# Keeping Silu results in PSUM and fetching a third tree's leaves in a fused attention and tree feed-forward kernel

## The chip, the cores and the metric

The kernel runs on one NeuronCore of one Trainium2 chip. The metric is device time in microseconds (us) of one execution; lower is better. Engines are named as in the profile: PE (matrix multiply), DVE (vector), ACT (scalar), POOL (GpSimd), SP (issues DMAs).

## The reference

Input x is 2 sequences of 4096 tokens, 512 values each. Both layers are preceded by a layer norm and added to x.

```
query, keys, values = unit_projection(LN(x) @ W.T + b)      # fft, divide by |f| + 1e-8, ifft
x1 = x + unbind(cumsum(bind(keys, values), axis=1), query)  # products of spectra
logits = LN(x1) @ W_in.T + b_in          # 8 trees x 255 nodes
decisions = logits > 0                   # one path of 8 nodes per tree
out = x1 + (silu(logits) * on_path) @ W_out.T
```

Each tree has depth 7: 127 inner nodes and 128 leaves. A token walks from the root, right where the decision is 1. Only the 8 nodes on its path count, 7 inner ones and one leaf.

## The kernel before

The 8192 tokens are cut into 32 blocks of 256 tokens (two halves j of 128). In one step of the loop the feed-forward part of block i runs beside the attention part of block n = i + 1 and the layer norm of block n + 1. The loop body (`step`) is written out by hand for each engine, and each engine executes its own list in order; semaphores with counts link them. Nothing is planned at run time: the order in the code is the order of the work.

Attention: PE projects with weights already folded with the Fourier basis (`project`, L485: Q, K, V, each a real and an imaginary part of 24 matmuls into two banks; the next projection may begin a part only when ACT has evacuated it, `evac_re` L724, `evac_im` L731). ACT squares and takes roots (`square`, `root`), POOL adds squares (`sum_squares`), adds the epsilon and later multiplies the spectra: `bind` (four multiplications), then DVE's four scans (`running_sum`, the cumulative sum), then POOL's `unbind` (four), `z_sums` (two), ACT's `z_high` and POOL's `z_low`. PE transforms back (`transform_back`), and DVE folds the result into x1 (`residual`, L1248), computes the statistics and normalises it. ACT's `std` takes the square root of the variance. The transposes of the normalised block are DMAs of SP.

All large products are done with numbers split in two 16-bit parts: high (ACT) and low (DVE), three matmuls for each tile.

Feed-forward: a tree has two column tiles of 128 in the logits: tile 0 holds the inner nodes, tile 1 the leaves. `logits(i, t, c)` (L509) are 12 matmuls of 256 columns into half c of PSUM bank t % 4. DVE's `decide` (L1206) turns tile 0 into decisions; PE's `counts` (L536) adds to the bank, with these decisions and a path matrix, a large negative value for each node that is off the token's path, so that Silu gives 0 there. ACT's `silu` (L787) writes to the buffer `acts` in SBUF, a ring of three trees. `act_high` (L799) rounds that to 16 bits in `a_hi`; DVE's `act_low` (L1216, the instruction is L1220) forms the rest in `a_lo`. `down` (L574) multiplies by W_out for each half into banks 0 and 1, 3 matmuls of 512 columns for each of the 14 tiles. PE may refill a bank when Silu has read it (`act_ready`).

The leaves of trees 0 and 1 are not multiplied. Their counts still run over both tiles, and ACT's `leaf` (L756) makes a one-hot of the leaf from the second half; PE turns it into a row number (`leaf_rows_of`), ACT copies the numbers (`leaf_row_copy`), POOL fetches each token's row of weights, bias and output weights from HBM by indirect DMA (`fetch`, L1051, two DMAs for each tree). DVE's `leaf_dots` (L1225) forms the dot product of the row with the normalised token, ACT's `leaf_silu` (L776) its Silu, and DVE's `leaf_add` (L1237) adds Silu times the output row to x1. `result` (L1278) adds the output of `down`, and SP stores it. GATHERED names these trees; a gathered tree has one tile in `COLUMN`, `a_hi`, `a_lo` and the weights.

A few narrow steps handle the Nyquist term of the spectrum (`nyquist_...`), and `scale_and_shift` (L1112, its second instruction is L1117) makes `nb`, the shift of the next layer norm, from two columns.

## Time and profile before

| | us |
|---|---|
| median of 3 runs (lowest, highest) | 1973.29 (1971.39, 1976.88) |
| the profiled execution, its span | 1974.17, 1972.3 |
| PE busy | 1875.0 (95%) |
| DVE busy | 1659.9 (84%) |
| ACT busy | 1109.8 (56%) |
| POOL busy | 946.3 (48%) |

Busy is time in which an engine had an instruction in work. Matmuls overlap each other, so a busy PE is not one at its peak. The granted clock of PE was 0.987 on the mean over the span.

### The profile page before, as it was taken

The page shows a single profiled execution, that of the slowest core. Times are in us where ns is not written, and L with a number is a line of the kernel's source. Part 1 is how long each engine was busy: PE and PEld are TensorE (multiplying, and loading weights), DVE is VectorE, ACT ScalarE, POOL GpSimd, SP SyncE. Part 2 cuts the span into 40 slices and gives each one's busy share as a digit, 9 for nine tenths or more (in the row PEclk, how much of TensorE's full clock was granted, in tenths as well). Part 3 has the DMA queues.
Part 4 walks back from the last instruction along what each step waited for, and adds up shares of the span by engine and source line. Part 5 has one row for each costly group of instructions (what it writes and reads, how often), then busy time and mean ns, then how long its engine had stood idle before and what let it go on. Part 6 is the DMA issues. An engine that isn't in the chain of part 4 may idle for free.

```text
span 1972.3 us, 40210 instructions
## 1 busy us (share of the span) xinstructions
PE 1875.0 (95%) x14680; PEld 1410.1 (71%) x14680; DVE 1659.9 (84%) x2874; ACT 1109.8 (56%) x2151; POOL 946.3 (48%) x736
## 2 busy tenths in 40 slices
PE   8599999999999999999999999999999999999978
PEld 6477777777777777777777777677777777777755
DVE  4888888888888988888888888888888898887883
ACT  5566555566555556655556655556655555654543
POOL 1254445565444555444556444556544455544450
PEclk9799999999999999999999999999999999999999
DMA  8023223222223222322222222322232322231212
GB/s 278 11 81 92 75 75 96 64 85 85 87 66 92 75 80 80 96 74 75 86 74 83 88 75 75 96 64 85 85 87 66 92 75 80 80 95 56 84 54 65
DMA packets 181784, 163.18 MB, mean 83 GB/s; under 512 B 140160, under 2 KB 140800, under 8 KB 181760
## 3 DMA queue, kind: packets, MB, share of 16 engines
q1 hardware_dynamic: 163328, 95.48, 16.3%
q0 software_dynamic: 18432, 67.38, 11.0%
q8 instruction: 15, 0.25, 0.1%
q14 instruction: 9, 0.07, 0.0%
HBM read 95.72 MB, written 16.78 MB: 57 GB/s over the span
## 4 chain that ended last, share of the span: by engine, by line
PE 69%; DVE 15%; issue 9%; ACT 0%; another core or an unknown queue 0%; DVEq 0%; DMA 0%; SPq 0%; ACTq 0%
PE bank_l L590 29%; PE bank_p L480 24%; PE bank_l L530 10%; DVE arena L1145 5%; DVE dec L1213 3%; DVE arena L1133 2%; PE bank_i L480 2%; PE bank_l L540 1%; DVE arena L1139 1%; DVE arena L1151 1%; DVE arena L1220 1%; PE bank_i L559 0%; PE bank_i L560 0%; PE bank_i L561 0%; PE bank_i L558 0%
## 5 line engine op out<-in xcount | busy, mean ns | idle before, releaser
L530 PE MATMUL bank_l<-arena,win_mem 128*128 128x256 f16 x5376 | 625.7, 274 | 15.4 <-DMA arena<-xn_pair 14.1
L590 PE MATMUL bank_l<-wout_mem,arena 128*128 128x512 f16 x2688 | 590.7, 379 | 0.0
L530 PEld LDWEIGHTS bank_l<-arena,win_mem 128*128 128x128 f16 x5376 | 523.7, 99 | 79.2 <-DMA arena<-xn_pair 14.2
L480 PE MATMUL bank_p<-arena,wf_hi 128*128 128x256 f16 x3072 | 506.1, 273 | 2.3 <-ACT arena L741 2.3
L590 PEld LDWEIGHTS bank_l<-wout_mem,arena 128*128 128x128 f16 x2688 | 263.1, 98 | 303.7 <-issue 0.2
L480 PE MATMUL bank_p<-arena,wf_lo 128*128 128x256 f16 x1536 | 419.2, 273 | 0.0
L985 POOL TENSOR_TENSOR arena<-arena 128x512 f32<-128x512 f32 x96 | 121.8, 1269 | 594.9 <-ACT arena L750 594.9
L795 ACT ACTIVATE arena<-bank_l,bias_in,s_logit 128x256 f32<-128x256 f32 x448 | 227.3, 558 | 208.9 <-PE bank_l L540 202.0
L480 PEld LDWEIGHTS bank_p<-arena,wf_hi 128*128 128x128 f16 x3072 | 299.7, 98 | 37.4 <-ACT arena L741 2.6
L1220 DVE SCALAR_TENSOR_TENSOR arena<-arena,s_act 128x512 f16<-128x512 f32 (+1 forms) x256 | 216.5, 847 | 72.8 <-ACT arena L805 72.8
L1213 DVE TENSOR_SCALAR dec<-bank_l,thr,off 128x256 bf16<-128x256 f32 x256 | 132.6, 538 | 86.8 <-PE bank_l L530 86.2
L1233 DVE SCALAR_TENSOR_TENSOR arena<-arena 128x512 f32<-128x512 f32 x128 | 202.4, 1616 | 0.0
L1062 POOL DMA_INDIRECT arena<-in_leaf_rows,leaf_row x128 | 142.7, 1115 | 88.3 <-issue 56.3
L783 ACT ACTIVATE leaf_act<-leaf_dot,arena 128x1 f32<-128x1 f32 x128 | 30.7, 286 | 247.5 <-DVE arena L1233 247.5
L805 ACT ACTIVATE arena<-arena,s_act 128x512 f16<-128x512 f32 (+1 forms) x256 | 167.1, 669 | 3.2
L480 PEld LDWEIGHTS bank_p<-arena,wf_lo 128*128 128x128 f16 x1536 | 150.5, 98 | 17.5
L540 PE MATMUL bank_l<-dec,path 128*128 128x256 bf16 x512 | 98.2, 274 | 44.8 <-DVE dec L1213 43.1
L1117 DVE SCALAR_TENSOR_TENSOR nb<-mv,rs 128x2 f32<-128x2 f32 x30 | 133.1, 4438 | 1.0
L1133 DVE RECIPROCAL arena<-arena 128x256 f32<-128x256 f32 x64 | 111.3, 1739 | 2.0 <-POOL arena L990 2.0
L1033 POOL TENSOR_TENSOR arena<-arena 128x512 f16<-128x512 f32 x62 | 84.3, 1380 | 55.8 <-ACT arena L715 55.8
L907 ACT ACTIVATE odd<-bank_i 128x256 f32<-128x256 f32 x64 | 24.5, 383 | 151.4 <-PE bank_i L480 151.4
L1145 DVE RECIPROCAL arena<-arena 128x256 f32<-128x256 f32 x64 | 107.7, 1725 | 1.1
(178 smaller groups left out, 2669.3 us busy)
## 6 DMA issues: line engine op xcount, KB each, us to landing
arena<-in_x SPq DMA_DIRECT2D x32, 512.0 KB, 3.4
arena<-arena SPq DMA_DIRECT2D x32, 512.0 KB, 2.9
out<-arena SPq DMA_DIRECT2D x64, 256.0 KB, 2.1
wout_mem<-in_w_in_t SPq DMA_DIRECT2D x1, 3584.0 KB, 15.4
arena<-in_w_out_t SPq DMA_DIRECT2D x1, 3584.0 KB, 14.0
arena<-xn_pair SPq DMA_TRANSPOSE x128, 2.7
arena<-in_leaf_rows,leaf_row POOLq DMA_INDIRECT x128, 4.8
win_mem<-in_wq SPq DMA_DIRECT2D x1, 1024.0 KB, 8.5
```

The costliest lines, as they stand in the source:

```text
L480: mm = pe.matmul(bank, a, b, start=(n == 0), stop=(n == len(pairs) - 1))
L530: mm = pe.matmul(bank_l[t % 4][:, c * T:(c + 1) * T], a[:, k, w:w + P], x2t[:, :, b, k, :], start=(c == 0 and k == 0 and m == 0), stop=((t ...
L590: mm = pe.matmul(bank_l[j][:, :], a[:, m, tok], w[:, m, :], start=(m == 0 and a is a_hi and w is wout_hi), stop=(m == DENSE - 1 and a is a ...
L795: ins = act.activation(acts[:, t % HELD, c * T:(c + 1) * T], bank_l[t % 4][:, c * T:(c + 1) * T], ACT.Silu, bias=bias_in[:, c, t:t + 1], s ...
L805: act.activation(a_hi[:, m:m + wide, :], acts[:, t % HELD, 0:wide * T].rearrange("p (c t) -> p c t", c=wide), ACT.Copy, scale=s_act[:, 0:1 ...
L1062: pool.indirect_dma_start(fetched[:, g, j, :], None, leaf_rows, bass.IndirectOffsetOnAxis(leaf_row[:, g, j:j + 1], 0)).then_inc(leaf_fetch ...
L1117: dve.scalar_tensor_tensor(out=nb1[:, :], in0=mv1[:, :, 0], scalar=-1.0, in1=rs1[:, :], op0=ALU.mult, op1=ALU.mult).then_inc(ln1_shift, 1)
L1133: dve.reciprocal(mag[:, Q, h], mag[:, Q, h]).then_inc(rinv_ready, 1)
L1145: dve.reciprocal(mag[:, V, h], mag[:, V, h]).then_inc(kv_rinv_ready, 1)
L1213: dve.tensor_scalar(dec[:, t % HELD, :], bank_l[t % 4][:, 0:T], thr[:, t:t + 1], off[:, 0:1], ALU.is_gt, ALU.mult).then_inc(dec_ready, 1)
L1220: dve.scalar_tensor_tensor(out=a_lo[:, m, :], in0=acts[:, t % HELD, 0:wide * T].rearrange("p (c t) -> p c t", c=wide), scalar=s_act[:, 0:1 ...
L1233: ins = dve.scalar_tensor_tensor(out=row, in0=row, scalar=1.0, in1=xn2[:, j, :], op0=ALU.mult, op1=ALU.mult, accum_out=leaf_dot[:, g, j:j ...
```

## The change

- GATHERED becomes (0, 1, 2): the leaves of tree 2 are fetched as well. DENSE falls from 14 tiles to 13, and each place that loops over gathered trees has a third turn. One round still covers all of them: one index copy after three one-hots.
- Silu writes its result over its input in the PSUM bank; both splits read it there. `acts` is gone, and with it Silu's waits for a free place in it. PE waits for `a_lo_ready` in place of `act_ready` before it refills a bank.
- The steps of PE, ACT, POOL and DVE stand in another order.

```diff
-GATHERED = (0, 1)
+GATHERED = (0, 1, 2)
-ROUNDS = ((0, 1),)
+ROUNDS = ((0, 1, 2),)
@@ PE, logits: a bank is free when the low split has read it
-                    pe.wait_ge(act_ready, TREES * i + t - 3)
+                    pe.wait_ge(a_lo_ready, TREES * i + t - 3)
@@ PE, down
-                pe.wait_ge(act_ready, TREES * i + 5 + j)
+                pe.wait_ge(a_lo_ready, TREES * i + 5 + j)
@@ PE, step
                 logits(i, 0, 0)
+                if attn:
+                    nyquist_rows(n)
                 logits(i, 1, 0)
+                counts(i, 0)
                 logits(i, 2, 0)
-                counts(i, 0)
-                if attn:
-                    nyquist_rows(n)
+                logits(i, 3, 0)
+                logits(i, 3, 1)
                 counts(i, 1)
-                logits(i, 2, 1)
-                logits(i, 3, 0)
+                counts(i, 2)
+                logits(i, 4, 0)
                 leaf_rows_of(i, 0)
-                logits(i, 3, 1)
-                logits(i, 4, 0)
                 logits(i, 4, 1)
                 logits(i, 5, 0)
-                counts(i, 2)
+                counts(i, 3)
                 logits(i, 5, 1)
                 logits(i, 6, 0)
-                counts(i, 3)
+                counts(i, 4)
                 logits(i, 6, 1)
-                counts(i, 4)
+                if attn:
+                    nyquist_sums(n)
                 counts(i, 5)
                 logits(i, 7, 0)
                 counts(i, 6)
-                if attn:
-                    nyquist_sums(n)
                 logits(i, 7, 1)
@@ ACT, silu
-                if t >= HELD:
-                    act.wait_ge(a_lo_ready, TREES * i + t + 1 - HELD)
-                elif not isinstance(i, int) or i:
-                    act.wait_ge(a_lo_ready, TREES * i)
-                    ins = act.activation(acts[:, t % HELD, c * T:(c + 1) * T], bank_l[t % 4][:, c * T:(c + 1) * T],
-                                         ACT.Silu, bias=bias_in[:, c, t:t + 1], scale=s_logit[:, 0:1])
+                    part = bank_l[t % 4][:, c * T:(c + 1) * T]
+                    ins = act.activation(part, part, ACT.Silu, bias=bias_in[:, c, t:t + 1], scale=s_logit[:, 0:1])
@@ ACT, step (the new order from evac_im(n, K) on, waits of the first block left out)
+  evac_im(n,K) root(n,Q) evac_re(n,V) square(n,K) evac_im(n,V) square(n,V) nyquist_size(n) root(n,K)
+  leaf(0) std(n+1) root(n,V) silu(0) act_high(0) leaf(1) leaf(2) silu(1) act_high(1) leaf_row_copy
+  silu(2) act_high(2) shifted(n+1) high(n+1) silu(3) act_high(3) silu(4) act_high(4) silu(5) act_high(5)
+  silu(6) silu(7) act_high(6) act_high(7) z_high(n) leaf_silu(0) leaf_silu(1) leaf_silu(2)
-  evac_im(n,K) root(n,Q) square(n,K) evac_re(n,V) evac_im(n,V) square(n,V) root(n,K) root(n,V) std(n+1)
-  leaf(0) leaf(1) silu(0) silu(1) nyquist_size(n) leaf_row_copy act_high(0) act_high(1) silu(2) act_high(2)
-  silu(3) act_high(3) silu(4) silu(5) act_high(4) shifted(n+1) act_high(5) silu(6) high(n+1) act_high(6)
-  silu(7) act_high(7) leaf_silu(0) z_high(n) leaf_silu(1)
@@ POOL, step
+                fetch(i, 0)
                 fetch(i, 1)
                 if attn:
                     bind(n)
-                fetch(i, 0)
+                fetch(i, 2)
                 if attn:
                     unbind(n)
@@ DVE, act_low
-                                         in0=acts[:, t % HELD, 0:wide * T].rearrange("p (c t) -> p c t", c=wide),
+                                         in0=bank_l[t % 4][:, 0:wide * T].rearrange("p (c t) -> p c t", c=wide),
@@ DVE, step (the order after the layer norm of block i)
+  q_inverse(0) next_stats decide(0) nyquist_den nyquist_inverse decide(1) q_inverse(1) kv_denominator
+  nyquist_unit decide(2) act_low(0) decide(3) kv_inverse(0) scale_and_shift act_low(1) kv_inverse(1)
+  nyquist_bind decide(4) act_low(2) k_scale low_of(n+1,0) act_low(3) decide(5) decide(6) act_low(4)
+  act_low(5) decide(7) running_sum low_of(n+1,1) act_low(6) nyquist_unbind nyquist_carry act_low(7)
+  leaf_dots(0) leaf_dots(1) carries leaf_add(0) leaf_dots(2) leaf_add(1) leaf_add(2) result(0) result(1)
-  next_stats q_inverse(0) decide(0) decide(1) q_inverse(1) kv_denominator kv_inverse(0) kv_inverse(1)
-  act_low(0) k_scale act_low(1) decide(2) decide(3) scale_and_shift decide(4) nyquist_den nyquist_inverse
-  nyquist_unit nyquist_bind act_low(2) decide(5) decide(6) act_low(3) running_sum act_low(4) decide(7)
-  nyquist_unbind act_low(5) act_low(6) act_low(7) leaf_dots(0) low_of(n+1,0) low_of(n+1,1) nyquist_carry
-  leaf_dots(1) leaf_add(0) carries leaf_add(1) result(0) result(1)
```

The lists of ACT and DVE are the diff's lines written side by side.

## Rows read from the trace of the kernel before

**Rows 1.** Waits of PE: who it waited for, us in total, times, longest.
```profile
PE bank_l L540 <- DVE dec L1213: 43.1, 30, 2.0
```

**Rows 2.** Timeline of DVE, the same step of three blocks: start us, us, engine, line.
```profile
101.54 0.17 DVE L1101 RECIPROCAL rs<-rs 128x2 f32<-128x2 f32 x1 [0.68 <-ACT rs L695]
...
923.46 0.17 DVE L1101 RECIPROCAL rs<-rs 128x2 f32<-128x2 f32 x1 [0.71 <-ACT rs L695]
...
1920.49 0.17 DVE L1101 RECIPROCAL rs<-rs 128x2 f32<-128x2 f32 x1 [0.36 <-ACT rs L695]
```

**Rows 3.** Timeline of PE over one block (adjacent instructions merged).
```profile
914.03 0.22 PE L480 MATMUL bank_i<-tab_hi,arena 128*128 128x129 f16 x1
...
915.39 0.38 PE L480 MATMUL bank_p<-arena,wf_hi 128*128 128x256 f16 x2
...
931.11 4.09 PE L530 MATMUL bank_l<-arena,win_mem 128*128 128x256 f16 x36
...
950.00 0.39 PE L540 MATMUL bank_l<-dec,path 128*128 128x256 bf16 x2 [1.42 <-DVE dec L1213]
...
954.09 2.75 PE L590 MATMUL bank_l<-wout_mem,arena 128*128 128x512 f16 x12
...
956.90 15.70 PE L590 MATMUL bank_l<-wout_mem,arena 128*128 128x512 f16 x72
...
972.44 0.22 PE L480 MATMUL bank_i<-tab_hi,arena 128*128 128x129 f16 x1
```

**Rows 4.** Timeline of ACT in the same block.
```profile
923.14 0.28 ACT L695 ACTIVATE rs<-mv,ln_eps 128x2 f32<-128x2 f32 x1
...
923.45 0.84 ACT L727 ACTIVATE arena<-bank_p,bias_f 128x256 f32<-128x256 f32 x2
...
964.03 0.48 ACT L783 ACTIVATE leaf_act<-leaf_dot,arena 128x1 f32<-128x1 f32 x2 [5.15 <-DVE arena L1233]
...
964.41 0.61 ACT L715 ACTIVATE arena<-arena 128x512 f16<-128x512 f32 x1
```

**Rows 5.** Timeline of POOL in the same block.
```profile
940.21 1.23 POOL L1062 DMA_INDIRECT arena<-in_leaf_rows,leaf_row  x1 [0.99 <-issue]
...
942.71 1.27 POOL L1008 TENSOR_TENSOR arena<-arena 128x512 f32<-128x512 f32 x1
...
953.72 1.69 POOL L1018 TENSOR_TENSOR arena<-arena 128x512 f32<-128x512 f32 x1 [3.43 <-DVE arena L1196]
...
961.63 1.71 POOL L1026 TENSOR_TENSOR arena<-arena 128x512 f32<-128x512 f32 x1
```

**Rows 6.** Timeline of DVE: three instructions of two columns.
```profile
943.22 4.45 DVE L1117 SCALAR_TENSOR_TENSOR nb<-mv,rs 128x2 f32<-128x2 f32 x1
...
954.76 0.21 DVE L1178 SCALAR_TENSOR_TENSOR sp_z<-bank_i,sp_carry,sp_hat 128x2 f32<-128x2 f32 x1
...
1763.98 4.90 DVE L1173 TENSOR_TENSOR sp_kv<-sp_hat 128x2 f32<-128x2 f32 x1
```

**Rows 7.** Four lines of DVE, 200 to 1900 us: ns min/median/max.
```profile
L1213 DVE TENSOR_SCALAR dec<-bank_l,thr,off x232: 527/539/545, 230.2 to 1893.1; 128x256 bf16<-128x256 f32 x116
...
L1233 DVE SCALAR_TENSOR_TENSOR arena<-arena x117: 679/1632/1753, 199.6 to 1899.3; 128x512 f32<-128x512 f32 x117
...
L1220 DVE SCALAR_TENSOR_TENSOR arena<-arena,s_act x232: 384/746/1751, 237.8 to 1897.7; 128x512 f16<-128x512 f32 x87, 128x256 f16<-128x256 f32 x29
...
L1243 DVE SCALAR_TENSOR_TENSOR arena<-arena,leaf_act x116: 740/744/753, 207.5 to 1852.2; 128x512 f32<-128x512 f32 x116
```

**Rows 8.** Timeline of DVE: folding, scans, result; leaf additions of block 30.
```profile
915.38 0.28 DVE L1260 SCALAR_TENSOR_TENSOR arena<-bank_i,sp_z,odd 128x64 f32<-128x64 f32 x1 [0.40 <-ACT odd L907]
...
950.97 1.39 DVE L1193 TENSOR_TENSOR_SCAN arena<-arena,carry 128x256 f32<-128x256 f32 x2
...
971.32 0.75 DVE L1281 SCALAR_TENSOR_TENSOR arena<-bank_l,s_out,arena 128x512 f32<-128x512 f32 x1
...
1904.05 3.20 DVE L1243 SCALAR_TENSOR_TENSOR arena<-arena,leaf_act 128x512 f32<-128x512 f32 x2
```

More of the change, by code:

```diff
@@ L17 @@
 INNER = 127
-GATHERED = (0, 1)
+GATHERED = (0, 1, 2)
 LEAVES = len(GATHERED)
-ROUNDS = ((0, 1),)
+ROUNDS = ((0, 1, 2),)
+ROUND_OF = {g: rnd for rnd, part in enumerate(ROUNDS) for g in part}
 COLUMN = {}
@@ L75 @@
 FOLD_RING = 5
-ARENA = 26128
+ARENA = 26392
 def build(nc, x, wq, wk, wv, b_qkv, w_in_t, b_in_t, w_out_t, dft, eye, table_hi, table_lo, running_d,
@@ L159, in build @@
         a_lo = take(DENSE * T // 2).bitcast(F16).rearrange("p (m t) -> p m t", m=DENSE)
-        acts = take(HELD * 2 * T).rearrange("p (r t) -> p r t", r=HELD)
         fetched = take(LEAVES * J * ROW).rearrange("p (g j w) -> p g j w", g=LEAVES, j=J)
@@ L525, in logits @@
                     else:
-                        pe.wait_ge(act_ready, TREES * (i - 1) + 5 + t)
+                        pe.wait_ge(a_lo_ready, TREES * (i - 1) + 5 + t)
                 w = COLUMN[t, c] * P
@@ L805, in act_high @@
                 act.activation(a_hi[:, m:m + wide, :],
-                               acts[:, t % HELD, 0:wide * T].rearrange("p (c t) -> p c t", c=wide), ACT.Copy,
+                               bank_l[t % 4][:, 0:wide * T].rearrange("p (c t) -> p c t", c=wide), ACT.Copy,
                                scale=s_act[:, 0:1]).then_inc(a_hi_ready, 1)
@@ L926, in step @@
                     root(n, Q)
+                    evac_re(n, V)
                     square(n, K)
-                    evac_re(n, V)
                     evac_im(n, V)
                     square(n, V)
+                    nyquist_size(n)
                     root(n, K)
-                    root(n, V)
-                if nxt:
-                    std(n + 1, mv1, rs1, ln1_mv, ln1_std)
                 if isinstance(i, int) and i == 0:
@@ L938, in step @@
                 leaf(i, 0)
-                leaf(i, 1)
+                if nxt:
+                    std(n + 1, mv1, rs1, ln1_mv, ln1_std)
+                if attn:
+                    root(n, V)
                 if isinstance(i, int) and i == 0:
@@ L943, in step @@
                 silu(i, 0)
+                act_high(i, 0)
+                leaf(i, 1)
+                leaf(i, 2)
                 silu(i, 1)
-                if attn:
-                    nyquist_size(n)
+                act_high(i, 1)
                 leaf_row_copy(i, 0)
-                act_high(i, 0)
-                act_high(i, 1)
                 silu(i, 2)
                 act_high(i, 2)
+                if nxt:
+                    shifted(n + 1)
+                if nxt:
+                    act.wait_ge(x2t_ready, 16 * J * (i + 1))
+                    high(n + 1, xn1, ln1_done, xn1_hi_ready)
                 silu(i, 3)
@@ L954, in step @@
                 silu(i, 4)
+                act_high(i, 4)
                 silu(i, 5)
-                act_high(i, 4)
-                if nxt:
-                    shifted(n + 1)
                 act_high(i, 5)
                 silu(i, 6)
-                if nxt:
-                    act.wait_ge(x2t_ready, 16 * J * (i + 1))
-                    high(n + 1, xn1, ln1_done, xn1_hi_ready)
+                silu(i, 7)
                 act_high(i, 6)
-                silu(i, 7)
                 act_high(i, 7)
-                leaf_silu(i, 0)
                 if attn:
                     z_high(n)
+                leaf_silu(i, 0)
                 leaf_silu(i, 1)
+                leaf_silu(i, 2)
             steps(act, first, step)
@@ L1051, in fetch @@
             def fetch(i, g):
-                known, added, stored = held(len(ROUNDS) * i + g // 2 + 1), held(LEAVES * i), held(16 * J * i)
+                known, added, stored = held(len(ROUNDS) * i + ROUND_OF[g] + 1), held(LEAVES * i), held(16 * J * i)
                 pool.wait_ge(consts_done, 1)
@@ L1489, in step @@
                     wout_low(3)
+                if attn:
+                    q_inverse(n, 0)
                 if nxt:
                     next_stats(n + 1)
+                decide(i, 0)
                 if attn:
-                    q_inverse(n, 0)
-                decide(i, 0)
+                    nyquist_den(n)
+                    nyquist_inverse(n)
                 decide(i, 1)
```

51 lines of the change are left out of this document (26 added, 25 removed).

## The prediction, made before the changed kernel was run

> **What bounds the kernel now.** I read the views in this order. The waits of PE come first: apart from start and end it waits in one place, the count of tree 5, for DVE's decision, 43.1 us over 30 blocks [rows 1]. The timeline of PE over one block then gives its own work. Projections run from 915.39 to 931.11, 15.72 us for 144 matmuls of 256 columns, 0.109 us each. The logits stage runs from there to 954.09, 22.98 us, with the wait of 1.42 us in it. The output matmuls (12, the count of tree 7, 72) take 18.35 us to 972.44; the 72 last ones took 15.54, 0.216 each. The back transform takes 1.36 us (914.03 to 915.39). Together 58.41 us, the distance from 914.03 to 972.44 [rows 3]. Of this 57.0 is work. The whole kernel is 31 such periods: 1818.95 us from the first to the last block, 58.68 on the mean [rows 2]. So PE is the bound, but DVE is hardly looser: in this block it starts folding at 915.38 [rows 8], with the transform's end, and the first result of the block before the next comes at 971.32, one us before the next transform begins at 972.44. The reader is to see in rows 6 and 7 what fills DVE. The dot products of L1233 take 679 ns alone and 1632 ns on the median; they run beside POOL's unbinding. L1117, two columns wide, took 4.45 us while POOL's four bind multiplications ran from 942.71.
>
> **The change part by part.**
>
> *Third gathered tree, PE.* One column tile leaves the logits (12 matmuls x 0.109 = 1.31 us) and the output (3 per half, 6 x 0.216 = 1.30 us). Two tiny leaf-row matmuls come, 0.05. With the wait of 1.42 gone, PE's own sum is 58.41 - 1.42 - 1.31 - 1.30 + 0.05 = 54.4 us [rows 3]. If PE stayed the bound, this would be all.
>
> *Third tree, DVE.* Two more dot products (2 x 0.68 to 2 x 1.63), two more additions (1.4 alone, 3.20 beside POOL [rows 7, 8]); the split of tree 2 halves, 0.75 to 0.4. Net +2.4 to +6.1 us a block, at the very end of the block.
>
> *Silu results stay in PSUM.* The low split (L1220) read two SBUF operands and took 746 ns on the median, up to 1751 beside POOL [rows 7]. With one operand in PSUM the nearest rows are the result, 0.75 [rows 8], and sp_z, which has its first operand in PSUM: 0.21 us at 954.76, in the middle of POOL's first unbinding multiplication (953.72, 1.69) [rows 5, 6]. Both operands in SBUF and as narrow: 4.45 and 4.90 [rows 6]. So I take 0.75 for each wide split, not held; the bounds are -1.0 (the excess of a held one) and +4.5 each. Result against leaf addition, 750 to 744 ns [rows 7, 8], shows no price for the PSUM operand itself. Two rules of the Trainium skill bear on this. SBUF — State Buffer, section "Who interferes with whom": a DVE instruction with two SBUF inputs contends with a GpSimd one that reads SBUF, one with at most one does not. By it rival C below is out; the rows show it for a two-column instruction only, so C stays in. Against the change speaks the Trainium skill's VectorE: DVE Perf Modes, section on the TRN2 errata, with 120 fixed cycles from PSUM against 58 from SBUF: about 0.06 us a split, 0.5 a block, an estimate from that page; if all of it lay on the path, the sum would be 16 us more. The trace shows 0.01 of it. Silu and the high split on ACT change place and not size; bounds 0.1 us either way each, none on the path that sets the end.
>
> *The price in PSUM* is that a bank is free after the low split, not after Silu. Tiles 4 to 7 and the output halves wait for it. By the new order PE comes to tree 4 some 8 us after tree 0's logits; the split of tree 0 is done then but for about 0.2 us, tree 1's likewise. I charge 0.4 us with the Nyquist rows, which now stand behind one logits tile and wait some tenths for ACT's last evacuation.
>
> *nb moves in front of the bind.* L1117 is now issued before the k scale that starts the bind, with only fetches on POOL: 4.45 goes to 0.16 [rows 6]. The decision behind it and with it PE's wait of 1.42 are freed. sp_kv moves there too. Nothing narrow with two SBUF inputs is left under the bind.
>
> *Indices at once, two fetches before the bind.* A pair of indirect DMAs with its start-up is 3.5 us of POOL (940.21 less 0.99, to 942.71) [rows 5]. Two pairs stand before the bind, so it starts about 6 us after the index copy (the start-up of 0.99 counted once, as it follows a wait) instead of 3.5, and ends about when the last decision allows the scans. Cost nothing, with 0.2 us of cover. The third pair runs under the scans.
>
> *ACT: z_high in front of leaf_silu(0).* POOL no longer waits there for a dot product. But leaf_silu(0), and with it the first leaf addition on DVE, now waits until POOL has finished unbinding and summing. In the block shown leaf_silu(0) ran at 964.03 in front of z_high [rows 4].
>
> *The ring.* With PE at 54.4, this chain is longer. It runs once round per block:
> 1. DVE folding to ACT's square root of the variance: 915.38 to 923.14, 7.8 us [rows 4, 8].
> 2. ACT: that root, then the evacuation of K, behind it in its queue, to 924.29: 1.15 [rows 4]. Only then may PE start the V projection.
> 3. PE: V projection 5.24; logits stage 22.98 - 1.42 - 1.31 + 0.05 = 20.3; waits 0.4, last result 0.2: 26.1 [rows 3].
> 4. DVE: decision 0.5, four scans 2.6: 3.1 [rows 7, 8].
> 5. POOL: unbinding and sums, 953.72 to 963.34: 9.6 [rows 5]. It meets DVE's dot products as it does now.
> 6. ACT: z_high 1.1, leaf_silu 0.48: 1.6 [rows 4].
> 7. DVE: first additions, half held, 2.5 (between 1.4 and 3.2); dots of the third tree, unheld, 1.3; two pairs of additions 2.7; two results 1.4: 7.9 [rows 7, 8].
> Sum 57.2 us. That is 2.8 above PE's sum: PE will idle about 2 us before the V projection (in the block shown the evacuation ended at 924.29, and PE's third projection was due at 915.39 + 2/3 of 15.72 = 925.87: 1.6 us to spare) and some tenths at the transform, which waits for POOL's z_low.
>
> **The sum.** 58.68 - 57.2 = 1.5 us a period, x 31 = 46. The last block, without attention, is PE's: 1.3 + 1.3 = 2.6. Set-up handles one fourteenth fewer weight columns, taken as 0. The profiled execution took 1974.17 (span 1972.3, 1.9 around it): 1974.2 - 49 = **1925 us**. The median of the runs shown, 1973.29, is 0.9 lower, within their spread.
>
> **Rivals.**
> *A: PE sets the end.* If steps 5 and 7 shrink by 2.5 us because POOL and DVE meet less (unheld they would be 7.5 and 6.8), the period is 54.4 + 0.4 = 54.8: 31 x 3.9 + 2.6 = 124, 1850 us. For: the splits no longer delay POOL. Against: dots now start right at the unbinding and their median is 1632 ns [rows 7].
> *B: the fetches delay the bind.* If two pairs cost 7.0 and not 6, or the index copy comes late, the scans wait; each us is 31. With 1 us the ring is 58.2 and the time 1956; with 1.5, no change. For: only 0.2 us of cover. Against: between its two DMAs POOL in rows 5 lost no such start-up (1.23 + 0.94 busy in 2.50).
> *C, slower: the PSUM split is held all the same.* The split of tree 3 stands beside the bind. If one operand in SBUF is enough to be held as L1117 was, 4.45 us, then tree 7's logits wait for the bank, the ring grows by about 4 and the period is 61.2: 1974 + 31 x 2.5 - 3 = 2049. It decides from 1.5 us of hold a block. For: L1117 and L1173 show how long a hold can be. Against: sp_z, not held.
> *D: the change does not remove what it says*, a table load more on ACT from Relu behind Silu: 2 x 1.3 us, hardly on the ring; in B's range.
>
> **How the numbers follow.** Forecast 0.60, A 0.15, B with D 0.15, C 0.10. A measurement tells about 0.3%, 6 us, from no change. Faster: forecast, A and two thirds of B, 0.85; same 0.04; slower 0.11. Step 7's unknown hold (1.1 either way), step 5 (1.5 down) and the handovers (0.5) make 1880 to 1955 for the forecast itself; towards A and B the range is 1866 to 1962.
>
> **What would show it.** Per block: PE waiting near 2 us before the V projection's real half for ACT's evacuation (L727), no wait of 1.42 at a count; L1117 at 0.16; splits at 0.75 beside the bind; leaf_silu(0) behind z_high with DVE idle 2 to 3 us before the first leaf addition; dots of the third tree at 0.68. Wrong if PE shows no idle (A), if DVE waits for POOL before the scans (B), or if a split shows over 1.5 us (C).

## The result, and the profile after

The changed kernel took 1980.72 us (median of 11 runs, 1979.48 to 1985.31), the kernel before 1975.48 (11 runs, 1971.26 to 1978.04). The ratio is 1.0031, 95% interval 1.0024 to 1.0039: slower by a third of a per cent, where 1925 was forecast. The profiled execution has a span of 1977.6 us, 5.3 more than before, and a mean granted clock of 0.976 against 0.987.

The waits of PE first (who it waited for, us in total, times, longest). The 43.1 us at a count [rows 1] are gone. Two other waits have come.

```profile
PE bank_p L480 <- ACT arena L726: 80.2, 30, 2.7
PE bank_l L530 <- DMA arena<-xn_pair: 36.5, 18, 18.1
...
PE bank_i L551 <- ACT arena L740: 7.4, 14, 4.2
```

The first is the idle time ahead of the V projection that the forecast expected (near 2 us a block; it is 2.67). The second falls between V's projection and the first logits (18.1 of it is set-up, the other 17 waits are 1.1 each on the mean); the forecast had nothing there.

PE over two blocks. The V projection starts in the first row of each pair, the logits in the second:

```profile
929.11 0.39 PE L480 MATMUL bank_p<-arena,wf_hi 128*128 128x256 f16 x2 [2.68 <-ACT arena L726]
...
936.05 1.48 PE L530 MATMUL bank_l<-arena,win_mem 128*128 128x256 f16 x12 [1.41 <-DMA arena<-xn_pair]
...
987.93 0.39 PE L480 MATMUL bank_p<-arena,wf_hi 128*128 128x256 f16 x2 [2.67 <-ACT arena L726]
...
994.85 0.38 PE L530 MATMUL bank_l<-arena,win_mem 128*128 128x256 f16 x2
```

6.94 us and 6.92 us between them, for different reasons: the first block waits 1.41 for the transposes of the normalised x2, the second waits for nothing but takes 6.92 us for 48 matmuls that need 5.24. The same core by windows around the second pair shows why (behind the window and its length: busy us and instructions of PE, PE's weight loads, DVE, ACT and POOL; then the granted clock, DMA share and GB/s):

```profile
985.00:987.90 2.90, 0.26 (x3) 0.00 (x0) 2.36 (x8) 1.02 (x3) 0.00 (x0) 1.00 0.45 181
987.90:990.00 2.10, 2.07 (x14) 1.64 (x15) 1.78 (x4) 1.93 (x4) 0.00 (x0) 0.73 0.23 80
990.00:992.00 2.00, 2.00 (x12) 1.35 (x10) 0.00 (x0) 1.12 (x3) 0.69 (x1) 0.50 0.97 256
992.00:994.85 2.85, 2.85 (x27) 2.51 (x25) 2.83 (x3) 1.78 (x3) 0.56 (x1) 0.95 0.72 129
```

PE had been busy for 0.26 of 2.90 us; then the clock is granted at 0.50, which is 1.2 GHz, and comes back to 2.4 within the projection. The clock falls so in 13 of the 28 blocks 1 to 28, though the idle time is 2.67 to 2.68 us in all of them; what decides in which is not shown.

The rest of one ring, in four timelines. DVE starts folding, ACT takes the root and evacuates K:

```profile
920.34 0.28 DVE L1258 SCALAR_TENSOR_TENSOR arena<-bank_i,sp_z,odd 128x64 f32<-128x64 f32 x1 [0.41 <-DVE arena L1279]
```

```profile
928.04 0.29 ACT L694 ACTIVATE rs<-mv,ln_eps 128x2 f32<-128x2 f32 x1 [4.39 <-DVE mv L1095]
928.24 0.82 ACT L726 ACTIVATE arena<-bank_p,bias_f 128x256 f32<-128x256 f32 x2
...
969.19 0.63 ACT L714 ACTIVATE arena<-arena 128x512 f16<-128x512 f32 x1 [8.45 <-POOL arena L1023]
```

DVE again: nb, one of the splits beside the bind, the last decision with the scans behind it, the additions, and the next folding:

```profile
945.77 0.16 DVE L1115 SCALAR_TENSOR_TENSOR nb<-mv,rs 128x2 f32<-128x2 f32 x1
...
954.11 0.75 DVE L1218 SCALAR_TENSOR_TENSOR arena<-bank_l,s_act,arena 128x512 f16<-128x512 f32 x1 [1.07 <-ACT arena L800]
...
956.41 0.54 DVE L1211 TENSOR_SCALAR dec<-bank_l,thr,off 128x256 bf16<-128x256 f32 x1
956.87 1.39 DVE L1191 TENSOR_TENSOR_SCAN arena<-arena,carry 128x256 f32<-128x256 f32 x2
...
970.74 2.42 DVE L1241 SCALAR_TENSOR_TENSOR arena<-arena,leaf_act 128x512 f32<-128x512 f32 x2 [1.56 <-ACT leaf_act L782]
...
979.16 0.28 DVE L1258 SCALAR_TENSOR_TENSOR arena<-bank_i,sp_z,odd 128x64 f32<-128x64 f32 x1 [0.41 <-DVE arena L1279]
```

POOL: the last bind multiplication and the first unbinding one:

```profile
955.18 1.26 POOL L1008 TENSOR_TENSOR arena<-arena 128x512 f32<-128x512 f32 x1
...
959.62 1.62 POOL L1015 TENSOR_TENSOR arena<-arena 128x512 f32<-128x512 f32 x1 [0.63 <-DVE arena L1194]
```

From 920.34 to 979.16 are 58.82 us; over blocks 1 to 28 the period is 58.85 on the mean, 58.66 before. nb fell from 4.45 us [rows 6] to 0.16, the splits stay at 0.75 beside the bind, DVE idles 1.56 us before the first leaf addition (2 to 3 were forecast): the signs came nearly as forecast, and yet no time is won.

### The profile page after: what moved, and what is told of

Read it like the earlier page. It is cut to its first block and busy times, and to the rows that moved or that the text cites. A ratio compares the mean times of both kernels' runs of the same rounds, so it can differ in the third digit from the quotient of the medians.

```text
span 1977.6 us, 39731 instructions
## 1 busy us (share of the span) xinstructions
PE 1819.7 (92%) x14168; PEld 1361.8 (69%) x14168; DVE 1587.4 (80%) x3066; ACT 1104.9 (56%) x2215; POOL 995.2 (50%) x800
## 5 line engine op out<-in xcount | busy, mean ns | idle before, releaser
L530 PE MATMUL bank_l<-arena,win_mem 128*128 128x256 f16 x4992 | 593.2, 273 | 36.6 <-DMA arena<-xn_pair 36.5
L530 PEld LDWEIGHTS bank_l<-arena,win_mem 128*128 128x128 f16 x4992 | 481.3, 98 | 102.7 <-issue 21.6
L590 PE MATMUL bank_l<-wout_mem,arena 128*128 128x512 f16 x2496 | 549.2, 379 | 0.0
L791 ACT ACTIVATE bank_l<-bank_l,bias_in,s_logit 128x256 f32<-128x256 f32 x416 | 209.1, 532 | 126.3 <-PE bank_l L540 121.9
L1059 POOL DMA_INDIRECT arena<-in_leaf_rows,leaf_row x192 | 199.2, 1038 | 140.0 <-issue 105.9
L1218 DVE SCALAR_TENSOR_TENSOR arena<-bank_l,s_act,arena 128x512 f16<-128x512 f32 (+1 forms) x256 | 165.8, 648 | 89.4 <-ACT arena L800 87.0
L1241 DVE SCALAR_TENSOR_TENSOR arena<-arena,leaf_act 128x512 f32<-128x512 f32 x192 | 166.7, 907 | 51.7 <-ACT leaf_act L782 48.3
L987 POOL TENSOR_SCALAR arena<-arena,eps_s 128x512 f32<-128x512 f32 x64 | 45.1, 704 | 236.8 <-ACT arena L753 234.1
L800 ACT ACTIVATE arena<-bank_l,s_act 128x512 f16<-128x512 f32 (+1 forms) x256 | 151.8, 607 | 6.2
L749 ACT ACTIVATE arena<-arena 128x1024 f32<-128x1024 f32 x96 | 101.7, 1060 | 5.3
```

What stands on the lines that cost most here:

```text
L530: mm = pe.matmul(bank_l[t % 4][:, c * T:(c + 1) * T], a[:, k, w:w + P], x2t[:, :, b, k, :], start=(c == 0 and k == 0 and m == 0), stop=((t ...
L590: mm = pe.matmul(bank_l[j][:, :], a[:, m, tok], w[:, m, :], start=(m == 0 and a is a_hi and w is wout_hi), stop=(m == DENSE - 1 and a is a ...
L791: ins = act.activation(part, part, ACT.Silu, bias=bias_in[:, c, t:t + 1], scale=s_logit[:, 0:1])
L800: act.activation(a_hi[:, m:m + wide, :], bank_l[t % 4][:, 0:wide * T].rearrange("p (c t) -> p c t", c=wide), ACT.Copy, scale=s_act[:, 0:1] ...
L1059: pool.indirect_dma_start(fetched[:, g, j, :], None, leaf_rows, bass.IndirectOffsetOnAxis(leaf_row[:, g, j:j + 1], 0)).then_inc(leaf_fetch ...
L1218: dve.scalar_tensor_tensor(out=a_lo[:, m, :], in0=bank_l[t % 4][:, 0:wide * T].rearrange("p (c t) -> p c t", c=wide), scalar=s_act[:, 0:1] ...
```

## The experiments

Sixteen kernels, run in four groups with the kernel before beside each. The median of the kernel before was 1967.1 to 1975.5 us in them, so kernels of different groups are best compared by the ratios. "Legs" below are means over blocks 1 to 28 of the times between the same steps as above: folding to first logits, logits to unbinding, unbinding to z_high, z_high to first leaf addition, that to the next folding. In the kernel after they are 15.51, 23.8, 9.57, 1.55 and 8.41.

| kernel | time, us | ratio to before (95%) | period |
|---|---|---|---|
| after | 1980.7 | 1.0031 (1.0024 to 1.0039) | 58.85 |
| a_std | 1981.9 | 1.0053 (1.0036 to 1.0069) | 58.94 |
| a_leaf | 1977.7 | 1.0034 (1.0021 to 1.0046) | 58.92 |
| a_load | 1962.8 | 0.9951 (0.9933 to 0.9969) | 58.30 |
| b_narrow | 1918.7 | 0.9728 (0.9712 to 0.9744) | 56.86 |
| d_two | 1931.9 | 0.9824 (0.9807 to 0.9840) | 57.37 |
| b_psum | 2021.4 | 1.0281 (1.0264 to 1.0298) | 60.05 |
| c_order1 | 2158.1 | 1.0970 (1.0951 to 1.0988) | 65.08 |
| c_order2 | 2154.1 | 1.0952 (1.0934 to 1.0970) | 64.80 |
| e_fetch | 1980.8 | 1.0056 (1.0039 to 1.0073) | 58.97 |
| e_scan | 2023.8 | 1.0280 (1.0260 to 1.0300) | 60.38 |
| e_ring2 | 2018.4 | 1.0248 (1.0231 to 1.0266) | 60.22 |
| e_ring | 2022.4 | 1.0266 (1.0247 to 1.0285) | 60.35 |
| f_warm | 1968.0 | 0.9998 (0.9989 to 1.0008) | 58.59 |
| f_warm_load | 1952.9 | 0.9923 (0.9900 to 0.9946) | 58.11 |
| f_all | 1951.2 | 0.9911 (0.9889 to 0.9933) | 58.10 |
| f_nb | 2160.9 | 1.0975 (1.0950 to 1.1000) | 64.86 |

### What each part of the change is worth

**b_narrow**: the kernel before with one move only, on DVE (the diff shows where the steps now stand; the same lines go from behind k_scale).

```diff
                 act_low(i, 0)
                 if attn:
+                    nyquist_den(n)
+                    nyquist_inverse(n)
+                    nyquist_unit(n)
+                    nyquist_bind(n)
+                if nxt:
+                    scale_and_shift(n + 1)
+                if attn:
                     k_scale(n)
```

> The kernel before with one edit on DVE: the four Nyquist steps and nb (scale_and_shift) stand in front of the k scale, so that no two-column instruction with both operands in SBUF is issued while POOL binds. Theory that the hold of 4.45 us of nb under the bind is what made PE wait 1.42 us at the count of tree 5: the wait goes, period 58.66 to 57.2, 1975.5 - 44 = 1931 (1925 to 1940). Rival, the hold comes to whatever DVE instruction stands beside the bind (decision or split): no change, 1975.

Measured 1918.72 us, below the expected range. The narrow instruction that took 4.45 us now comes ahead of the bind:

```profile
918.23 0.16 DVE L1117 SCALAR_TENSOR_TENSOR nb<-mv,rs 128x2 f32<-128x2 f32 x1
...
922.88 1.23 DVE L1220 SCALAR_TENSOR_TENSOR arena<-arena,s_act 128x512 f16<-128x512 f32 x1 [1.54 <-ACT arena L805]
```

and PE is without a gap, at full clock, over the 1500 us from 200 to 1700 (the first pair of numbers after the window's length is PE):

```profile
200.00:1700.00 1500.00, 1500.00 (x11989) 1138.21 (x11987) 1257.50 (x2310) 874.60 (x1742) 796.72 (x602) 1.00 0.28 83
```

The period is 56.9 us, what PE has to do with two gathered trees. The rival is true in part: the split in the second row, both operands in SBUF, stands beside the bind and takes 1.23 us, but PE does not wait for it. This one move, also part of the change, gains 2.7% and beats both kernels. So everything else in the change costs about 3% of the time, 60 us by the ratios.

**d_two**: the kernel after with two gathered trees, everything else as it is.

```diff
-GATHERED = (0, 1, 2)
+GATHERED = (0, 1)
-ROUNDS = ((0, 1, 2),)
+ROUNDS = ((0, 1),)
 ...
                 logits(i, 2, 0)
+                logits(i, 2, 1)
 ...
-                fetch(i, 2)
-                leaf_dots(i, 2)
-                leaf_add(i, 2)
-                leaf(i, 2)
-                leaf_silu(i, 2)
```

> The kernel after with its third tree's leaves dense again (two gathered trees, no third fetch, no leaf_dots(2), leaf_add(2), leaf_silu(2), and logits(2,1) back); the PSUM results and the new order stay. Theory 1 (one ring per block: folding, root, V projection, logits, decision and scans, unbind and sums, z_high, leaf additions): the last leg loses one pair of additions, 2.9 us, and its dots, 1.7 us partly, and the logits stage between V projection and the last decision gains one logits step of some 1.3 us, so the period falls from 58.9 to about 56 to 57.5 us: 1885 to 1935 us. Theory 2 (PE sets the end, or the third tree is what saves time): PE gets 1.3 to 1.5 us a block more to do, so the time rises to about 2015 to 2025 us. If GpSimd's fetch was what held the block, the time falls by the fetch's 3 us a block, to 1885.

Measured 1931.93: theory 1 holds, theory 2 falls. PE has more to do, and the period is 1.5 us shorter, the time 2.1%. The 2.68 us ahead of V's projection are gone and no wait of PE in the blocks is above a few tenths:

```profile
PE bank_l L530 <- DMA arena<-xn_pair: 15.2, 2, 14.4
PE bank_i L551 <- ACT arena L741: 12.5, 31, 4.6
```

The last leg is 5.76 us (8.41 with three trees), unbinding to z_high 9.15 (9.57). The third tree takes 2.6 us of work from PE [rows 3], which then idles, and puts 3.1 on the ring.

**b_psum**: b_narrow with the Silu results left in PSUM, order unchanged.

```diff
-                    pe.wait_ge(act_ready, TREES * i + t - 3)
+                    pe.wait_ge(a_lo_ready, TREES * i + t - 3)
 ...
-                    ins = act.activation(acts[:, t % HELD, ...], bank_l[t % 4][:, ...], ACT.Silu, ...)
+                    part = bank_l[t % 4][:, c * T:(c + 1) * T]
+                    ins = act.activation(part, part, ACT.Silu, ...)
```

> The kernel before with the narrow VectorE steps ahead of k_scale (1918.7 us in the run before) and in addition the Silu results kept in PSUM, nothing else. Theory 1: the splits read PSUM beside the bind and cost no more, the banks are given back about 2 us later than by Silu alone but PE does not wait for them: 1910 to 1925 us. Rival (the bank held until its split stops the logits, the slower case of the prediction): PE waits for a split at four to six logits steps of a block, 1 to 3 us in all, and the time rises to 1950 to 2010 us.

Measured 2021.35, 3.2 us a period above b_narrow: the rival's mechanism, at a price above the rival's range. PE waits for splits three times a block:

```profile
PE bank_l L529 <- DVE arena L1215: 88.1, 95, 1.9
```

```profile
1026.60 1.48 PE L529 MATMUL bank_l<-arena,win_mem 128*128 128x256 f16 x12 [1.28 <-DVE arena L1215]
```

```profile
1025.79 0.75 DVE L1215 SCALAR_TENSOR_TENSOR arena<-bank_l,s_act,arena 128x512 f16<-128x512 f32 x1 [2.25 <-ACT arena L800]
```

The split is not held, it takes 0.75; it is the bank that is held until ACT's high split and DVE's low split, each in its queue, are through. With the new order most of this is gone (d_two is 0.5 us a period above b_narrow), but there is no gain. No kernel has the new order with the Silu results in SBUF, so that half us is not divided between the two.

### The legs of the ring, one at a time

**a_std**:

```diff
-                std(i, mv2, rs2, ln2_mv, ln2_std)
                 if attn:
                     evac_re(n, K)
+                std(i, mv2, rs2, ln2_mv, ln2_std)
```

> The changed kernel with one edit on ACT: the evacuation of K's real part stands in front of the square root of the second layer norm. PE's wait of 2.7 us before the V projection goes, and with it the half clock that follows it in about half of the blocks. Ring theory as predicted (the V projection is on the ring): 1.5 us a block, 1934. Ring theory as the changed kernel's trace suggests (the logits wait for the transposes by DMA anyway, 15.1 to 15.8 us after the folding starts, with or without the half clock): the wait moves to the logits, only the 0.3 us a block that half-clock blocks lose goes, 1980.7 - 8 = 1973 (1968 to 1980). Rival, the clock is the cause: period 58.2 or less in all blocks, 1960.

No gain, and 2 us above the highest of the three ranges. The wait has only changed its place and its releaser: the second half of V's projection needs K's imaginary part evacuated, and that stands behind the norm's high split. The idle time is as long as before and the clock falls as often (15 of 28 blocks). Folding to logits stays 15.57.

```profile
989.82 0.39 PE L480 MATMUL bank_p<-arena,wf_hi 128*128 128x256 f16 x2 [2.79 <-ACT arena L740]
```

**a_leaf**:

```diff
-                if attn:
-                    z_high(n)
                 leaf_silu(i, 0)
                 leaf_silu(i, 1)
+                if attn:
+                    z_high(n)
                 leaf_silu(i, 2)
```

> The changed kernel with one edit on ACT: leaf_silu(0) and leaf_silu(1) stand in front of z_high again. Ring theory: DVE's first leaf additions no longer wait for POOL's sums (in the changed kernel DVE idles 1.56 us there, after a held narrow instruction); the additions of trees 0 and 1 move ahead, partly held by POOL, and about 0.9 us of each of 31 periods goes: 1980.7 - 29 = 1952 (1945 to 1960). Rival, DVE is simply overfull (the sum of its instructions with their holds sets the period, whatever the order elsewhere): no idle to recover, within 6 us of the changed kernel.

1977.7 us: no gain (1.0034 to before, the kernel after 1.0031). The last two legs fall from 9.96 to 9.22, and folding to logits grows from 15.5 to 16.3. So the ring theory's leg came and its gain did not, and the rival names the right time for another reason. DVE's last step of x1 takes 0.69 us for the first half; that of the second half is now issued during POOL's sum of squares and takes longer, and so does the sum (1.27 alone):

```profile
862.21 0.69 DVE L1273 SCALAR_TENSOR_TENSOR arena<-arena 128x512 f32<-128x512 f32 x1
...
865.02 1.64 DVE L1273 SCALAR_TENSOR_TENSOR arena<-arena 128x512 f32<-128x512 f32 x1
```

```profile
864.17 1.93 POOL L982 TENSOR_TENSOR arena<-arena 128x512 f32<-128x512 f32 x1 [9.49 <-ACT arena L749]
```

**a_load**: the load of the next x (SP) from ahead of the two x2 transposes to behind them, and its statistics behind the first decision (DVE).

```diff
+                decide(i, 0)
                 if nxt:
                     next_stats(n + 1)
-                decide(i, 0)
```

> The changed kernel with the load of the next x issued behind the two transposes of the second layer norm, not ahead of them, and DVE's statistics of it behind the first decision. Theory that the transposes are late because they share the DMA engines with this load: landing falls from 3.7 to near 2.7 us, the logits start at 14.0 to 14.7 us after the folding (then set by the V projection), about 0.8 us a block in blocks without the half clock, 1980.7 - 15 = 1966 (1955 to 1975); the blocks with the half clock gain little. Rival, the transposes are slow of themselves: no change.

1962.8: folding to logits is 15.04 on the mean, most blocks 14.9. Against the 14.2 us that the forecast's steps 1 to 3 come to, 1.3 were missing on the mean, and this is a third of them. It is not all the transposes' doing. They land 3.2 us after their issue in place of 3.6 to 3.8, and the clock falls in only 4 of the 28 blocks, against 13, with the same idle time of 2.68. A block in which it falls has a period of 59.3 us in both kernels, one in which it does not 58.5 in the kernel after and 58.1 here: by these numbers more than half of the 0.55 us that the period loses is the clock's. Why it falls less often is not shown.

**f_warm**: 20 matmuls whose result nobody reads, in the idle time.

```diff
                     project(n, K)
+                    for _ in range(20):
+                        pe.matmul(bank_l[2][:, 0:T], wf_hi[:, K, 0, 0:P], xt[:, :, 0, 0, :], start=True, stop=True)
                     project(n, V)
```

> The kernel after with 20 extra matmuls of 128x256 (about 2.2 us, results unused) between K's and V's projection, where TensorE idles 2.7 us; the start of V's projection stays where it is. Theory 1 (V's projection runs at half clock because TensorE had idled): no block has it any more and V's projection takes 5.3 us in each; the logits then wait for the x2 transposes in every block, so fold to logits falls only from 15.5 to about 15.2 us: 1966 to 1978 us. Theory 2 (the half clock has another cause, such as the load on the whole chip): the slow blocks stay, 1978 to 1985 us.

Theory 1 holds, though folding to logits was to fall to 15.2 and did not. More work for PE makes the kernel 0.33% faster (0.9998 to 1.0031), the clock falls in none of the 28 blocks, the mean granted clock goes back from 0.976 to 0.987, and now every block waits for the transposes instead (31 waits; 18 before, set-up among both):

```profile
PE bank_l L530 <- DMA arena<-xn_pair: 52.5, 31, 18.1
PE bank_p L480 <- ACT arena L728: 14.9, 30, 0.5
```

```profile
984.26 0.39 PE L480 MATMUL bank_p<-arena,wf_hi 128*128 128x256 f16 x2 [0.50 <-ACT arena L728]
...
991.09 1.15 PE L530 MATMUL bank_l<-arena,win_mem 128*128 128x256 f16 x9 [1.30 <-DMA arena<-xn_pair]
```

Folding to logits is hardly shorter, 15.47. The gain comes from behind: logits to unbinding is 23.57 in all blocks, as against 24.06 on the mean in those of the kernel after where the clock had fallen. The clock itself is at 1.00 again in that leg. But the logits start right behind V's projection in these blocks, and PE stops at the Nyquist rows for ACT's last evacuation, which the wait for the transposes covers in the others. In the kernel after, in its second block shown above:

```profile
996.59 0.60 PE L551 MATMUL bank_i<-running,sp_raw 96*128 96x3 f32 x4 [0.26 <-ACT arena L740]
```

From the first logits to those of tree 1, behind these rows, PE takes 2.20 us in this block (994.85 to 997.05) and 1.69 in the one at 936.05 (to 937.74): the whole half us.

**f_warm_load**: both together.

> As f_warm, with the load of the next x behind the two transposes and its statistics behind the first decision. Theory 1: fold to logits 14.8 to 14.9 us in every block (15.5 in the kernel after, 15.04 with the later load alone), period 58.0: 1950 to 1958 us. Rival (the two costs are one, the later load already took it all): 1960 to 1965 us.

1952.88, period 58.11, folding to logits 14.95: the two nearly add (in ratio to before, the load alone is worth 0.80%, the filled gap alone 0.33%, both 1.08%, 21 us). With the clock up in every block the later load is worth 0.49 us a period (58.59 to 58.11). The transposes still end the wait, by 0.64 us:

```profile
981.38 1.48 PE L530 MATMUL bank_l<-arena,win_mem 128*128 128x256 f16 x12 [0.64 <-DMA arena<-xn_pair]
```

**f_all**: f_warm_load with a_leaf's move.

> As f_warm_load, and the first two leaf silus ahead of z_high. If the legs add, 0.7 us a block less than f_warm_load: 1930 to 1938 us. If x1's last step is held beside GpSimd's sum of squares again, as when this was done alone: no change against f_warm_load.

1951.19, no change against f_warm_load (intervals overlap): -0.74 in the last two legs, +0.72 from folding to logits, as in a_leaf.

### Moves inside the changed order that gave nothing or cost

**e_fetch**:

```diff
                 fetch(i, 0)
-                fetch(i, 1)
                 if attn:
                     bind(n)
+                fetch(i, 1)
                 fetch(i, 2)
```

> The kernel after with the second tree's fetch issued behind the bind instead of ahead of it, nothing else. In the kernel after the bind ends within 0.1 us of VectorE's last decision, and the scans follow both. Theory 1 (the scans wait for the decision that waits for the last logits, so for PE): no gain, 1972 to 1982 us. Theory 2 (GpSimd's fetches hold the bind and so the ring): the bind ends 1.5 us a block earlier and all of it is gained, 1925 to 1940 us.

No gain, theory 1. The fetch that moved comes back behind the bind: logits to unbinding +0.76, unbinding to z_high, which no longer runs beside so many dot products, -1.25, z_high to first addition +0.53.

**e_scan**:

```diff
+                if attn:
+                    running_sum(n)
                 decide(i, 7)
-                if attn:
-                    running_sum(n)
-                if nxt:
-                    low_of(n + 1, 1, xn1, xn1_hi_ready, xn1_lo_ready)
```

with e_fetch's order, and low_of(n + 1, 1) directly behind low_of(n + 1, 0).

> As e_fetch, and the scans moved ahead of the last decision (the second part of the norm's split moved out from between them and the dots, directly behind the first part). Theory 1 (the ring: folding, V projection, logits, scans, unbind, additions): logits to unbind falls from 23.8 to about 22.2 us, period 57.3, 1920 to 1935 us. Rival (VectorE's own queue between the scans and the results is full, so an earlier scan only makes the additions wait for fetches and dots): under 0.5 us a block, 1962 us or more.

Both theories missed; 43 us slower than e_fetch. The scans ended at 977.7, but POOL was still issuing the two fetches that now stand behind the bind:

```profile
976.37 1.36 DVE L1194 TENSOR_TENSOR_SCAN arena<-arena,carry 128x256 f32<-128x256 f32 x2
```

```profile
977.50 0.98 POOL L1059 DMA_INDIRECT arena<-in_leaf_rows,leaf_row  x1 [0.30 <-issue]
978.78 0.94 POOL L1059 DMA_INDIRECT arena<-in_leaf_rows,leaf_row  x1 [0.30 <-issue]
979.74 1.29 POOL L1015 TENSOR_TENSOR arena<-arena 128x512 f32<-128x512 f32 x1
```

Unbinding starts 2 us after the scans' end, and the last decision, which PE's last count needs, comes 2.7 us later than it could; PE waits 0.83 us for it. This leg grows by 0.8 us against e_fetch, and folding to logits by 0.6, which was not traced to a cause. **e_ring2** (with a_load's move) and **e_ring** (with a_leaf's too) repeat it:

> As e_scan, and the load of the next x behind the two transposes with its statistics behind the first decision. If the legs add: 0.55 us a block less than e_scan, 16 us. If PE has become the bound by then: no change against e_scan.

> As e_ring2, and the first two leaf silus ahead of z_high. Alone on the kernel after this moved the time by nothing, since x1's last step was then held beside GpSimd's sum of squares. If that hold stays: no change against e_ring2; if the ring is shifted away from it: 0.7 us a block less, 22 us, so 1880 to 1895 us.

2018.4 and 2022.4: the later load is worth 5 us here, not 16; leaf silu first, nothing.

**c_order1, c_order2**: all engines reordered at once, with a_load's later load.

```diff
+                if nxt:
+                    next_stats(n + 1)
                 if attn:
                     q_inverse(n, 0)
-                if nxt:
-                    next_stats(n + 1)
+                    q_inverse(n, 1)
+                    nyquist_den(n)
+                    nyquist_inverse(n)
                 decide(i, 0)
...
                 leaf_dots(i, 0)
+                if nxt:
+                    low_of(n + 1, 1, xn1, xn1_hi_ready, xn1_lo_ready)
```

> All three trees and the PSUM results of the kernel after, with another order of all engines: std of the norm between K's real and imaginary evacuation, the narrow VectorE steps ahead of k_scale, the bind between the first two fetches, load of the next x behind the transposes, first leaf silu ahead of z_high. Theory 1 (the ring): its legs become 15 (fold to logits), about 21 (logits to unbind), 9.6, 1.0 and 8.5: period 55.2 us, 31 x 3.65 = 113 us less than the kernel after: 1860 to 1880 us. Theory 2 (the time is lost on PE's half clock and the third tree's work, whatever the order): no more than the 15 us that the later load brought: 1955 to 1975 us.

> As c_order1 with a different order in VectorE's queue (dots of the first tree and the norm's splits late, scale_and_shift directly ahead of the narrow steps, next_stats first) and ScalarE's (Silu of each tree at once followed by its high split). Theory 1 (the ring): period 55.3 us, 1862 to 1885 us; theory 2: 1955 to 1975 us.

Missed by nearly 300 us. I had moved the load back and put its statistics at the head of DVE's queue, which waits there 5.9 us a block for the load:

```profile
DVE st L1101 <- DMA arena<-in_x: 175.5, 30, 7.1
```

and one of the norm's splits met the four unbinding multiplications (1048.89 to 1053.81) and was held over all of them:

```profile
1048.59 5.77 DVE L1133 TENSOR_TENSOR xn_pair<-arena,xn_pair 128x512 f16<-128x512 f32 x1
```

They say nothing of the ring. That these two places cost the time is read from the first kernel's trace; neither was moved alone, and the second kernel's trace was not analysed.

**f_nb**: scale_and_shift back behind k_scale in the kernel after.

```diff
                     kv_inverse(n, 0)
-                if nxt:
-                    scale_and_shift(n + 1)
                 act_low(i, 1)
 ...
                     k_scale(n)
+                if nxt:
+                    scale_and_shift(n + 1)
                 act_low(i, 3)
```

> The kernel after with the next norm's scale and shift (nb, two columns) back behind k_scale, so under the bind, nothing else but the split that needs it behind it. Theory 1 (the hold of some 4.5 us is in VectorE's queue ahead of the last decisions, which are in the ring): 1 to 2 us a block more, 2005 to 2045 us. Rival (VectorE has enough slack there since the ring waits for the logits): 1978 to 1985 us.

2160.9, far above both ranges. It is not the hold: nb came 1.4 us ahead of the bind and took 0.16. In the changed order ACT does the next norm's shift ahead of the fourth Silu, and its whole queue stood behind it:

```profile
971.25 1.52 ACT L703 ACTIVATE arena<-arena,nb,rs 128x512 f32<-128x512 f32 x2 [3.61 <-DVE nb L1115]
```

```profile
978.33 0.61 PE L540 MATMUL bank_l<-dec,path 128*128 128x256 bf16 x2 [3.98 <-DVE dec L1211]
```

So this run does not price the hold inside the changed order; b_narrow does, in the order before.

## Why the prediction was wrong

The mechanism was right: no engine is full, one ring sets the period, and the last leg's additions are on it (d_two). What failed is the length of step 3 and the period that the ring was compared with. By its steps, forecast and, from the block above, measured:

| step | forecast | measured |
|---|---|---|
| 1 folding to the root | 7.8 | 7.70 |
| 2 root, K's evacuation | 1.15 | 1.07 |
| 3 V projection, until the logits start | 5.24 | 6.94 |
| 3, 4 logits to the scans (20.3 + 0.4 + 0.2 + 0.5) | 21.4 | 20.82 |
| 4, 5 scans to unbinding | 2.6 | 2.75 |
| 5 unbinding and sums | 9.6 | 9.57 |
| 6 z_high, leaf_silu | 1.6 | 1.55 |
| 7 additions, dots, results | 7.9 | 8.42 |
| sum | 57.3 (the prediction rounds to 57.2) | 58.82 |

**Step 3 is the one that failed**, by 1.7 us in this block and 1.5 on the mean. It took the stretch from V's projection to the logits as PE's own work, 48 matmuls at the rate of [rows 3]. That forgets two things. The logits need x2 normalised, split and transposed, a second path from the same root. In the kernel before it was hidden, because PE came to the logits later, but its length was there to be read. SP issues the two transposes of x2:

```profile
926.41 2.59 SPq L339 DMA_TRANSPOSE arena<-xn_pair  x2
```

and, of the same two, the median time from issue to landing:

```profile
arena<-xn_pair SPq DMA_TRANSPOSE x2, 2.7
```

The second is issued at 927.7 and lands 2.7 us later, 15.1 us behind the folding at 915.38; PE started the logits at 931.11 [rows 3], 15.7 behind it. The forecast's steps 1 to 3 put them at 14.2, ahead of the landing. In the kernel after, with the load of the next x issued 1.1 us ahead of the transposes and not 2.2, the landing is at 15.3 on the mean, and PE waits 0.8 to 1.5 us for it in the blocks at full clock. In the others PE, after its 2.67 us of idle time, runs the projection in part at the lower clock, for 6.9 us. Either alone fills the gap. Filling the idle time alone takes 0.04 us from this leg (f_warm), the later load alone 0.46 (a_load, with part of the clock's share in it), both 0.56. Some 0.9 us of the 1.5 stay in the best case tried, the length of the transpose path itself: the 5.24 was out of reach in every order tried. The clock has a second price, half a us in the logits stage, where PE reaches the Nyquist rows before ACT's last evacuation. The 0.4 that the forecast charged for this and for the banks it pays only in these blocks.

The Trainium skill's TensorE: Matmul & The Clock Gate, section "Part 1: The HAM clock gate", gives 1.2 and 2.4 GHz for the two states of the clock and says that an idle PE falls to the lower. The trace agrees: 0.50 and 1.00 granted, the lower one after the idle time. The forecast named the idle time and did not ask what comes of it.

**Step 7** was 0.5 short: 0.41 of it is the fold waiting for the block's own last result, which [rows 8] showed in another form (0.40 on ACT) and I had not counted. The other steps together were 0.7 too long.

**The sum's base.** The larger error was not in the ring. By the forecast's own numbers PE needs 57.0 us a block for two trees once the wait of 1.42 is gone, and the ring with three is 57.2. So the whole forecast gain was that of the narrow move, and the third tree and PSUM were already worth nothing in it. I compared the new ring with the old period and never with the old kernel less its one wait. b_narrow measures it: 56.9. Then the 2.2 us that steps 3 and 7 were short, less the 0.7 of the others, turn a forecast gain of 2.5% into a loss of 0.3%.

**Rivals.** C's mechanism, a split held like nb, did not come: 0.75 beside the bind. The Trainium skill's SBUF — State Buffer, section "Who interferes with whom", says that a DVE instruction with at most one SBUF input, outside its two-port modes, does not contend with GpSimd; the 0.75 agrees for the wide split as well. C's condition, a bank held too long, is real in another form: 3.2 us of period in b_psum. B did not decide: the bind behind two pairs ended at 956.44, the last decision at 956.95. A never came near, since PE was idle. D did not come: ACT loads a table 64 times in both kernels. Splits not held, nb at 0.16, leaf_silu behind z_high and the third tree's dots at 0.68 were as forecast. The range, 1866 to 1962, was too low because every term was taken from a kernel in which PE hides the paths beside it. It was also narrower than its own terms: the 1.1 and 0.5 us named for step 7 and the handovers, times 31, reach 1975.

What stays open: how far the x2 transposes would come down with no other transfer beside them, and whether three trees can beat b_narrow in any order. PE's work would allow it (it idles over 3 us a block); in the orders tried here the ring did not.

## What to carry to other kernels

When a change takes work off the engine that is the bound, list every path that this engine had hidden, to each place where it waits, and time them before counting the gain; taking one wait away shows the next, and an idle gap on TensorE can cost the clock as well. Price the parts of a bundled change one by one against the kernel before with its one visible wait removed: here a single move of five narrow steps was worth 2.7%, and the rest cost more than that. A result kept in a shared buffer saves nothing if its reader stands late in a queue.

## What the runs showed of the hardware

- A DVE instruction of two columns with both operands in SBUF waited through four back-to-back POOL multiplications: 4.45 us, 0.16 when moved away. It is not a matter of width: a 128x512 split with both operands in SBUF took 5.77 under the four unbinding ones, 0.69 alone. The dot products beside unbinding, as wide, took 1.74 in turn with POOL's 1.71; what decides between the two is not shown.
- After 2.67 us of idle PE, V's projection ran at a granted clock of 0.50 in part, in 13 of 28 blocks; 20 matmuls in the gap (0.50 us of it left) removed it.
- The x2 transposes took 2.7 us to land before, and 3.8 and 3.6 after (medians of the first and the second over blocks 1 to 28), where the load of the next x is issued 1.14 us ahead of them (2.16 before); with the load behind them (a_load) 3.2 and 3.1. DMA traffic beside them differs in more than this load, so it is not shown to be the only reason.
- The 128x512 split with one operand in PSUM took 0.75 us beside POOL's bind; with both in SBUF 1.23 there (b_narrow), 0.72 to 0.75 alone.
